# A graph network's second convolution sums two runs of edges a tile instead of reading ring copies

## What is computed

```python
def gcn_conv(x, W, b, src, dst, num_nodes):
    xw = x @ W
    s, d = concatenate([src, loop]), concatenate([dst, loop])
    deg = segment_sum(ones, d)
    norm = deg[s] ** -0.5 * deg[d] ** -0.5
    return segment_sum(norm[:, None] * xw[s], d) + b
h = relu(gcn_conv(x, W1, b1, src, dst, N))      # stage Gcn1
out = gcn_conv(h, W2, b2, src, dst, N)          # stage Gcn2
x = layernorm(x + out)                          # stage Gcn2
```

## Time and profile before

| | |
|---|---|
| median of 3 runs | 5244.6 us (5239.62 to 5244.79) |
| profiled execution | 5236.4 us, its span 5234.7 us |
| PE busy | 4230.7 us (81%) |
| VectorE busy | 3327.6 us (64%) |
| GpSimd busy | 3297.9 us (63%) |
| ScalarE busy | 2740.8 us (52%) |
| gathers from `y_t` (Gcn1 and Gcn2) | 784, 804.0 us |
| stage Gcn2, from its first index load to the next stage's | 2928.64 to 3526.68 us of the span |

### The profile page before, as it was taken

The page is one execution under the profiler, slowest core; times in us unless marked ns, Lnnn a source line. Parts: engine busy times, 40 slices in busy tenths (PEclk is TensorE's granted clock), DMA queues, the critical chain, the costliest instruction groups (busy, mean ns, idle before and its releaser), DMA issues. The chain is left out here.

```text
span 5234.7 us, 115742 instructions
## 1 busy us (share of the span) xinstructions
PE 4230.7 (81%) x31393; PEld 3749.4 (72%) x31394; DVE 3327.6 (64%) x6779; ACT 2740.8 (52%) x6900; POOL 3297.9 (63%) x3162
## 2 busy tenths in 40 slices
PE   2899999689999799887999555447888499999997
PEld 1788888588888699887999455445666377666765
DVE  5454454477777488785676577666888355565555
ACT  0455555444444488774444376665666244444444
POOL 1544444187777377756777577747777477777772
PEclk9999999899999899998999777768999799999999
DMA  1677777456666488776787566656777244444442
GB/s 30 204 227 232 235 226 233 156 201 225 221 218 218 172 265 266 250 235 224 271 277 268 156 190 186 192 160 185 220 224 222 74 114 122 114 123 116 115 115 90
DMA packets 442518, 990.98 MB, mean 189 GB/s; under 512 B 157141, under 2 KB 195957, under 8 KB 419960
## 3 DMA queue, kind: packets, MB, share of 16 engines
q1 hardware_dynamic: 341560, 872.37, 49.0%
q0 software_dynamic: 100800, 116.72, 10.8%
HBM read 452.11 MB, written 380.15 MB: 159 GB/s over the span
## 5 line engine op out<-in xcount | busy, mean ns | idle before, releaser
L735 PE MATMUL ps_all<-arena 128*128 x16000 | 2016.7, 285 | 554.0 <-DMA arena<-arena 384.3
L735 PEld LDWEIGHTS ps_all<-arena 128*128 128x128 f32 x16000 | 1983.2, 203 | 624.0 <-issue 623.8
L664 POOL DMA_INDIRECT arena<-n_t,ix_now x784 | 914.8, 1167 | 485.5 <-issue 226.6
L664 POOL DMA_INDIRECT arena<-y_t,ix_now x784 | 804.0, 1025 | 355.7 <-issue 241.0
L664 POOL DMA_INDIRECT arena<-x_rows,ix_now x392 | 375.1, 957 | 441.3 <-PE ps_all L735 303.7
L1097 ACT ACTIVATE arena<-bytes 128x2048 f32<-128x2048 uint8 (+1 forms) x300 | 476.1, 1619 | 307.7 <-DMA bytes<-pairs_d 209.8
L1606 PEld LDWEIGHTS ps_all<-w,tp 128*128 128x128 f32 x4000 | 478.5, 192 | 159.8 <-issue 118.8
L1606 PE MATMUL ps_all<-w,tp 128*128 128x128 f32 x4000 | 496.5, 277 | 71.0 <-ACT store_b L1740 38.9
L664 POOL DMA_INDIRECT arena<-x_t,ix_now x392 | 391.6, 999 | 182.2 <-issue 119.0
L694 DVE TENSOR_TENSOR arena<-iota,window 128x1024 f32<-128x1024 f32 x302 | 363.5, 1220 | 98.2 <-ACT bytes L1062 91.9
L1855 DVE SCALAR_TENSOR_TENSOR tmp<-ps_all,invdeg,load_a 128x128 f32<-128x128 f32 x800 | 225.2, 344 | 211.1 <-PE ps_all L735 188.6
(11 more groups left out here) (202 smaller groups left out, 7861.9 us busy)
## 6 DMA issues: line engine op xcount, KB each, us to landing
x_t<-store_a SPq DMA_DIRECT2D x150, 512.0 KB, 3.2
s_t<-store_a SPq DMA_DIRECT2D x50, 1024.0 KB, 3.9
n_t<-store_b SPq DMA_DIRECT2D x50, 1024.0 KB, 6.2
load_a<-s_t SPq DMA_DIRECT2D x50, 1024.0 KB
bytes<-pairs_d SPq DMA_DIRECT2D x100, 512.0 KB, 6.8
y_t<-store_b SPq DMA_DIRECT2D x100, 512.0 KB
load_b<-x_t SPq DMA_DIRECT2D x100, 512.0 KB
arena<-arena SPq DMA_DIRECT2D x147, 192.0 KB
```

Source lines behind the costliest of these rows:

```text
L664: pool.indirect_dma_start(out=slot_rows(at, W, pitch), out_offset=None, in_=table, in_offset=bass.IndirectOffsetOnAxis(ap=ix_now[:, at:at ...
L735: last = pe.matmul(out(j, 2) if wide else out(j, 1), hot, both(rows) if wide else rows, start=(k == 0), stop=(k == n - 1))
```

## The change

Gcn2 gets `two_windows` and `from_kept`. TensorE takes two runs for each tile, SP makes no ring copies. Group 0's matrices still come from VectorE, now as one 128x2048 compare instead of group 0's and group 1's 128x1024 ones; group 1's are widened by ScalarE from `pairs_d`, of which SP loads only group 1's half (256 KB a block). ScalarE widens three blocks ahead, between `norm_root` and `norm_apply`. In Update one `sem_inc` on SP between two waits goes.

```diff
@@ class Gcn2(Pass)
-        skew_lead = 3
+        two_windows = True
+        from_kept = True
+
+        def hot(self, ve, m, u, q, windows):
+            if q == 0 and windows and exists(m):
+                if not isinstance(m, int) or m >= 2:
+                    ve.wait_ge(S("agg0"), before(m - 1))
+                one_hots(ve, m, 0, self.hot_at(u), True)
+
+        def load_kept(self, sp, m, u):
+            sp.dma_start(bytes8[u][:, HOT:2 * HOT], pairs_d[bass.ds(m * P, P), HOT:2 * HOT]).then_inc(S(f"kept{u}"), 16)
+
+        def load_kept_first(self, sp):
+            for m in range(4):
+                if m >= 2:
+                    sp.wait_ge(S("hot1"), now(m - 2))
+                self.load_kept(sp, m, m % 2)
+
+        def load_kept_next(self, sp, m, u):
+            if exists(m + 4):
+                sp.wait_ge(S("hot1"), now(m + 2))
+                self.load_kept(sp, m + 4, u)
...
         def scalar_loop(self, act, windows):
+            for m in range(3):
+                self.widen_group(act, m, m // 2, m % 2, 1, windows)
             self.squares(act, 0, 0)
             super().scalar_loop(act, windows)
 
         def scalar(self, act, m, i, u, windows):
             norm_root(act, m)
+            self.widen_group(act, m + 3, i + 1 + u, 1 - u, 1, windows)
             self.stored(act, i, u)
             norm_apply(act, m, 0, self.pre(u), store_a[u])
...
@@ class Update(Pass), next_index
                 sp.wait_ge(S("ix"), landed("ix", c + 1, self.lists))
-                sp.sem_inc(S("copying"), 1)
                 self.load_index(sp, c + 2)
```

## The result

| | before | after |
|---|---|---|
| median of 4 runs | 5243.4 us | 5282.7 us |
| ratio, 95% interval | 1 | 1.0076 (1.0059 to 1.0094) |
| span of the profiled execution | 5234.7 us | 5274.3 us |
| Gcn2: first gather's start to last gather's end | 543.8 us | 588.9 us |
| Gcn2: last gather's end to the next stage's index load | 51.4 us | 41.1 us |

The kernel is 39 us slower. Held time is the sum of what the gathers take over 0.944 us. For "behind the compare" a gather counts if it ends 0.81 to 0.82 us after one. "Behind all" is over the whole stage, "behind the compare" over its middle; over the whole stage the latter went from 0.66 to 1.65.

What follows compares the result with a forecast made beforehand. GpSimd's gathers were taken to bound the second convolution. The longer compare's +39 us and the tail's -10 summed to +29, so 5273.6 us against 5244.6, range 5234 to 5310.

Steps and rivals of the forecast that it cites:

- The bound: Second convolution: GpSimd never waits, so its gathers set the pace, 1.398 us each, 11.18 us a block of 8.
- The compare: Second convolution: one 2048-wide compare holds gathers longer than the pair, +0.80 us a block (+0.21 to +1.46), +39 us.
- The formula 2.16 - x: Second convolution: a gather starting x us into the long compare is held 2.16 - x, x from 0 to 1.25.
- The tail: Second convolution's last gather to the next stage: without ring copies 12 to 7 us shorter, taken as -10.
- Matmuls, conversion, stored bytes: Second convolution: doubled matmuls, ScalarE's widening and 256 KB loads a block stay hidden under 11 to 12 us.
- above 0.85: Second convolution: TensorE's granted clock in the changed kernel's trace, up from a mean of 0.71.
- the copies had disturbed the gathers: Second convolution: without copies, pace falls to 10.57 us a block, 5205 us; part of the no-longer-holds rival, chance 0.18.
- the stored bytes set the pace: Second convolution, rival: the loop of stored bytes takes about 12.8 us a block, +68, 5313 us; chance 0.08.
- TensorE's clock does: Second convolution, rival: at a granted 0.6 a block takes 13.1 us, +83, 5328 us; chance 0.03.
- the -4 us worked out from it: Whole sum if the skill page's 115 ns held, the long compare then costing about 0.83 us a block.

Runs made afterwards that it cites:

- the four runs of the first chip: Changed kernel with compare in two, 5241.9 us; kernel before with one long compare, 5291.2; changed with iota in PSUM, 5211.3; that plus Update's compares halved, 5194.9.
- the first three experiments: Changed kernel with its compare made two of 1024, 5241.9 us; kernel before with one 2048-wide compare, 5291.2; changed kernel with iota in PSUM, 5211.3.
- the third: Changed kernel with its 2048-wide compare reading iota from a PSUM bank: 5211.3 us, 0.9935 of the kernel before.

## Why the prediction was right

*The bound.* GpSimd's gathers, by the row in which it never waits. Right: the stage's gathers grew by 45.1 us, held time by (1.93 - 0.97) x 49 = 47. Eight gathers take 12.1 us, 12.0 was foreseen.

*The compare.* The step that carried the sign. I took 1.5 us a block from the second SAGE layer, bounds 0.91 to 2.16; it was 1.73 in mid-stage. Over the whole stage the hold behind the compare grew by (1.65 - 0.66) x 49 = 48.5 us where I had 39. The gathers together grew by 45.1, since holds behind other instructions shrank by 1 to 2 us, and some 2 us I can't place. So this term is mis-sized, and 6 of the 10 us by which the change was larger than forecast (+39 for +29) come through it. The formula 2.16 - x was right, and the even spread of x was not: all 45 compares between 2960 and 3500 hold a gather, and 43 of the stage's 47 gathers of over 1.5 us start 0.2 us or 0.5 to 0.6 us into theirs; the mean of the 47 is 0.44, so 1.72. The same two values recur in the kernel before, where most held gathers of mid-stage start 0.20 to 0.22 or 0.51 to 0.60 us into the first compare of the pair (0.54 in the earlier trace rows), so I had the means to see that x isn't spread evenly. That it follows from VectorE's chain starting with the landing of the same gathers is argued, not shown.

*The tail.* Forecast -12 to -7, taken -10; 51.4 became 41.1. Right in its parts too: from the last gather's end to the first of the last three `norm_apply` 14.6 us for 12.0 (TensorE starts 2.64 after the gather, where I had estimated 1.5), then 8.10 and 8.09 for 8.1 twice, 2.76, and 7.5 for 7.6.

*Matmuls, conversion, stored bytes.* Each was costed at nothing, with its cover named, and together they cost next to nothing: the split compare with all three has gathers of 547.2 us for 543.8, and costs what the kernel before costs. The clock was granted at 0.81, under my "above 0.85", without a price, as a late TensorE costs nothing here.

*The rest* of the +39.6 us between the two spans: +45.1 and -9.3 from last gather to next gather leave 3.8, nearly all in the following stage (586.8 to 590.7 us). I had no term for it and didn't settle it; that stage takes 593 to 599 us in the four runs of the first chip, so it may be no more than how runs differ.

*Rivals.* That the copies had disturbed the gathers: against it are the kernel before with the long compare (slower by 45 with its copies unchanged), the split compare (no faster in its gathers without them) and the kernel before with iota in PSUM (gathers of 984 ns with them). That the stored bytes set the pace: 1.7 us of waits. That TensorE's clock does: GpSimd has no wait for sums in the changed kernel's mid-stage.

The Trainium skill's account (SBUF — State Buffer, "SBUF: two separate sides") of a lock that the loser waits for until VectorE's instruction ends agrees with the runs. Of its 115 ns the prediction said too much. The page's figure is for the end of the blocking, and a trace shows only the end of the gather, 0.81 to 0.82 us after the instruction; if the block lifted after 0.115, some 0.70 of a gather's 0.944 would be left, an estimate, and that fits as well. So the runs neither bear the figure out nor refute it, and the -4 us worked out from it rested on taking it for the gather's end. The same section names, as what takes the port against GpSimd, a VectorE instruction in a two-port mode, or one with two SBUF inputs if the GpSimd instruction reads SBUF, and in its box on DMAs issued by GpSimd the two-port modes alone. Here a plain f32 tensor-tensor compare with two SBUF inputs held them, and with one input in PSUM it didn't.

## What to carry to other kernels

Where GpSimd issues indirect DMAs without a pause, look at the longest VectorE tensor-tensor instruction with both inputs in SBUF: here one of 2.28 us, longer than the 1.25 us from gather to gather, stalled one every time, by up to 2.0 us. Move a small, constant input such as an iota to a free PSUM bank (71 us here), or cut the instruction into pieces (in two, 41 us; the four pieces of 0.70 us that hold gathers least were timed only where it made no difference). Merging two short instructions into one long one can cost more than the work it saves, and the cost shows on another engine. And before a whole time is held against a mechanism, see that the engine it slows is still the one that waits for nothing.

## What the runs showed of the hardware

- A gather of 128 rows took 0.944 us free and, in the second SAGE layer of the kernel before, up to 3.08 us when begun inside a compare of 2.28 us. It is blocked only if it starts after the compare has: one begun 0.33 us ahead of it was free.
- A VectorE f32 tensor-tensor instruction with both inputs in SBUF held every gather that began between 0.05 us after its start and 0.2 us before its end, in the traces of both kernels and in those of the first three experiments and of the four pieces; with one input in PSUM (the scalings in all of these, the compare in the third) it held none.
- The same compare, 128x2048 f32, takes 2.28 us from SBUF and SBUF and 2.28 to 2.29 us from PSUM and SBUF.
- The kernel before ran in 5246 us on one chip and in 6529 us on two others. There GpSimd waited, 83.0 us in 560 with iota in PSUM, for releases that the trace doesn't show, and the long compare in the kernel before, worth 45 us on the first chip, cost nothing that the times can tell (1.0004, 0.9988 to 1.0019).
